# Late feed-forward tiles of a routed decoder block in half tiles of 128 rows, two experts a step, first layer in whole fp32

## The chip, the cores and the metric

One Trainium2 chip, one NeuronCore. The metric is the device time of one execution in microseconds (us), the median of the runs; lower is better.

## The reference

A pre-norm decoder block in fp32 on x of 8 batches x 256 rows x 128 columns: self attention with a hyperbolic distance, cross attention to 512 context rows a batch, and a routed feed-forward. The last part is what matters here:

```python
logits = -dist2 + jnp.einsum('bld,ed->ble', x, rw) + rb
topv, topi = jax.lax.top_k(logits, TOP_K)            # 4 of 16 experts
w = jax.nn.softmax(topv, axis=-1)
hidden = jax.nn.gelu(jnp.einsum('bld,efd->blef', x, w1) + b1, approximate=False)   # 128 -> 512
exp_out = jnp.einsum('blef,edf->bled', hidden, w2) + b2                            # 512 -> 128
sel = jnp.take_along_axis(exp_out, topi[..., None], axis=2)
fused = jnp.sum(w[..., None] * sel, axis=2)
```

Each of the 2048 rows goes to 4 of 16 experts: 8192 (row, expert) pairs. With the reference's own inputs the experts get 795, 395, 564, 125, 242, 518, 21, 542, 789, 908, 478, 25, 1110, 287, 504 and 889 of them (counted on the reference's routing). In tiles of 256 rows, each with one expert, that is 42 tiles; in half tiles of 128 rows it is 73.

## The kernel before, in words

Attention runs first, batch after batch. While cross attention runs, each row is normalised, routed, and sent by POOL's indirect DMAs (L835) into a DRAM table `rows`, which has a region of 2048 rows for each expert; a row there is 130 floats (the row, where its result goes, its weight).

The feed-forward is a walk over `TILES` tiles (L39: 47, the most that any routing can need). Which expert and which start in `rows` a tile has is computed on DVE (`early_map`, `late_map`, `late_starts`) and read into registers by each engine (`tile_entry`). The first nine, `EARLY`, are full tiles of what was sent before the last batch; the others come when the last batch's rows have landed. With the inputs above, 33 of the 38 late tiles (t = 9 to 41) hold rows, and t = 42 to 46 are empty but walked all the same. For each tile t, and two or three tiles deep at once:

- SP, `load_tile` (L581 to L586): waits until the ring slot t mod 6 (`NR` = 6) is free, that is until both result DMAs of tile t-6 have landed (`rout`), reads the start into a register, and issues one DMA of 256 rows into `RIN`, two rows a partition.
- PE, `rows_turn` (L1494): two transposes of 128x128 into `tps`.
- ACT, `x_high` (L1117) and `stage_high` (L1123): the high parts of the rows and of the expert's 128x512 first weights, rounded to fp32r. DVE, `x_low` (L2132) and `stage_low` (L2125): the remainders.
- PE, `hidden` (L1504): 4 chunks x 3 fp32r matmuls (high x high, high x low, low x high) over 256 rows. ACT, `gelus` (L1133): 4 Gelus of 256 columns.
- PE, `outputs` (L1519): 2 x 4 fp32 matmuls of 128 columns; the trace has two MATMUL records for each fp32 matmul (x16).
- DVE, `weigh_out` (L2142, L2145): adds the bias, multiplies by the weight. POOL (L881): two indirect DMAs of 128 rows into the DRAM table `picks`.

The order of the work is written out by hand. PE's step t is: read the expert, transposes of tile t+2, `hidden` of t+1, `outputs` of t. ACT's is `x_high` and `stage_high` of t+1, then `gelus` of t. DVE's is `x_low`, `stage_low` of t+2, then `weigh_out` of t.

The end: SP has issued every `load_tile`, reads six counts of `DONE_I` (`real_tiles`, L599) that say how many tiles hold rows, waits until these tiles' results have landed (L602), and only then loads `picks` back in 16 DMAs (L605). PE and DVE add these to X, and SP writes `out`.

Of the kernel before, what the change touches and what calls it, by code (L numbers as in the profile page):

```python
# [26 lines left out]
P = 128  # L27
# [10 lines left out]
SLOTS = 256  # L38
TILES = (B * N * TOPK + E * (SLOTS - 1)) // SLOTS  # L39
RW = D + 2  # L40
# [52 lines left out]
def decoder_block(nc, a, out):  # L93
    with ExitStack() as ctx:
# [154 lines left out]
        def s_emptied(b, n):  # L249
# [21 lines left out]
        iota_i, iota_f = sB("iota_i", [E], I32), sB("iota_f", [E])  # L271
        step_i, step_f = sB("step_i", [8], I32), sB("step_f", [8])
        first_i, first_f = sB("first_i", [E], I32), sB("first_f", [E])
# [11 lines left out]
        NEXT = sB("NEXT", [E])  # L285
        CNT, CMP, TILE_N, LOW, LOWN, END = (sB("CNT", [E]), sB("CMP", [E, 8]), sB("TILE_N", [E]), sB("LOW", [E, E]),
                                            sB("LOWN", [E, E]), sB("END", [E]))
# [8 lines left out]
        wo_x, less_half = sB("wo_x", [D]), sB("less_half", [1])  # L296
        EARLY = 9

# [170 lines left out]
        def y_bank(t):  # L469

            return (ops[:, :, :].rearrange("p a n -> p (a n)"), bps[:, :])[0 if t < EARLY else t % 2]

        def y_free(t):

            return t if t < EARLY else t - 1

        def tile_row(t):

            return (MAPI[0], t) if t < EARLY else (MAPI[1], t - EARLY)

        def tile_entry(t, c):

            table, at = tile_row(t)
            return table[at:at + 1, c:c + 1]

# [13 lines left out]
        def _(sp):  # L499
# [81 lines left out]
            def load_tile(t):  # L581

                s = t % NR
                wait(sp, rout[s], 32 * (t // NR))
                at = sp.value_load(tile_entry(t, 1), min_val=0, max_val=(E + 1) * CAP - SLOTS)
                sp.dma_start(RIN[:, s], rows[bass.ds(at, SLOTS), :].rearrange("(p i) c -> p i c", i=2)).then_inc(rin[s], 16)  # L586
            for t in range(NR):
# [30 lines left out]
        def _(g):  # L618
# [152 lines left out]
            ch.step(g.iota(iota_i[:, :], pattern=[[1, E]], base=0, channel_multiplier=0))  # L771
            ch.step(g.iota(step_i[:, :], pattern=[[SLOTS, 8]], base=0, channel_multiplier=0))
            ch.step(g.iota(first_i[:, :], pattern=[[CAP, E]], base=0, channel_multiplier=0))
# [111 lines left out]
        def _(act):  # L885
# [233 lines left out]
            def stage_high(t):  # L1119

                e = act.value_load(tile_entry(t, 0), min_val=0, max_val=E - 1)
                wait(act, h_full, 2 * (t - 1))
                act.copy(W1h[:, t % 2, :], W1[:, bass.ds(e * FF, FF)]).then_inc(w1_high, 1)  # L1123
                return e
# [21 lines left out]
            for t in range(TILES):  # L1146
                if 0 < t < TILES - 1 and t != EARLY - 1:
                    x_high(t + 1)
                    at.append(stage_high(t + 1))
                if t == 3:  # L1150
                    t_copy("n3", B - 1)
                if t == 4:
                    half_tanh(B - 1)
                gelus(t, at[t])
                if t == EARLY - 1:
                    act.wait_ge(map_rdy, 2)
                    x_high(t + 1)
                    at.append(stage_high(t + 1))
            for i, (lo, hi) in enumerate(PE_PIECES):
# [4 lines left out]
        def _(pe):  # L1164
# [323 lines left out]
            def rows_turn(t):  # L1488

                s = t % NR  # L1490
                pe.wait_ge(rin[s], 16 * (t // NR + 1))
                wait(pe, x_lo, t - 1)
                for i in range(2):
                    ins = pe.transpose(tps[t % 2][:, i * P:(i + 1) * P], RIN[:, s, i, 0:D], ident[:, :])  # L1494
                ins.then_inc(rows_full, 1)

            def hidden(t):

                pe.wait_ge(x_lo, t + 1)
                pe.wait_ge(w1_low, t + 1)  # L1500
                wait(pe, h_rdy, FC * (t - 1))
                for c in range(FC):
# [7 lines left out]
            def outputs(t, e):  # L1510

                pe.wait_ge(h_rdy, FC * (t + 1))
                wait(pe, y_used, y_free(t))
# [3 lines left out]
                for i in range(2):  # L1517
                    for c in range(FC):
                        ins = pe.matmul(y[:, i * P:(i + 1) * P], HB[:, t % 2, c, i * P:(i + 1) * P],  # L1519
                                        W2[:, bass.ds(e * FC * D + c * D, D)], start=(c == 0), stop=(c == FC - 1))  # L1520
                ins.then_inc(y_full, 1)

            def tile_expert(t):
                return pe.value_load(tile_entry(t, 0), min_val=0, max_val=E - 1)

# [10 lines left out]
            for t in range(TILES):  # L1536
                if t == EARLY:
                    pe.wait_ge(map_rdy, 2)
                e = tile_expert(t)
                if t == EARLY - 1:  # L1540
# [24 lines left out]
        def _(dve):  # L1565
# [298 lines left out]

            def tile_starts(table):

                rch.link(dve.tensor_scalar(MAPF[:, 2:3], MAPF[:, 2:3], float(CAP // SLOTS - 1), float(SLOTS), ALU.min, ALU.mult))
                rch.link(dve.scalar_tensor_tensor(out=MAPF[:, 1:2], in0=MAPF[:, 3:4], scalar=float(CAP),
# [3 lines left out]
            def early_map():  # L1872
# [4 lines left out]
                                                  op0=ALU.add, op1=ALU.subtract))  # L1877
                rch.link(dve.tensor_tensor(CMP[:], CNT[:, :].unsqueeze(2).broadcast_to([P, E, 8]),
                                           step_f[:, :].unsqueeze(1).broadcast_to([P, E, 8]), ALU.is_gt))
                rch.link(dve.tensor_reduce(FULL[:, :], CMP[:], AX, ALU.add))  # L1880
                tile_ends(FULL, END)
# [3 lines left out]
                tile_experts(FULL)  # L1885
                tile_starts(MAPI[0])

            def late_map():

                dve.wait_ge(*t_emptied("pl", B - 1))  # L1890
                rch.link(dve.tensor_tensor(CNT[:, :], NEXT[:, :], first_f[:, :], ALU.subtract))
                rch.link(dve.tensor_tensor(CMP[:], CNT[:, :].unsqueeze(2).broadcast_to([P, E, 8]),
                                           step_f[:, :].unsqueeze(1).broadcast_to([P, E, 8]), ALU.is_gt))
                rch.link(dve.tensor_reduce(TILE_N[:, :], CMP[:], AX, ALU.add))
                rch.link(dve.tensor_tensor(TILE_N[:, :], TILE_N[:, :], TAKEN[:, :], ALU.subtract))
                tile_ends(TILE_N, END)

            def late_starts():
# [4 lines left out]
                rch.link(dve.tensor_reduce(PASTN[:, 0:1], PAST[:, :], AX, ALU.add))  # L1903
                rch.link(dve.tensor_tensor(MAPF[:, 2:3], MAPF[:, 2:3], PASTN[:, 0:1], ALU.add))
                tile_starts(MAPI[1])

            def real_tiles():

                rch.link(dve.tensor_scalar(DONE_F[:, :], END[:, E - 1:E], float(EARLY), None, ALU.add))
                rch.link(dve.tensor_tensor(ORD[:, :], ORD[:, :], DONE_F[:, :].broadcast_to([P, TURNS]), ALU.is_lt))  # L1910
# [218 lines left out]
            def x_low(t):  # L2129
# [3 lines left out]
                                  ALU.subtract).then_inc(x_lo, 1)  # L2133

            def weigh_out(t, e):

                s = t % NR
                dve.wait_ge(rin[s], 16 * (t // NR + 1))
# [3 lines left out]
                dve.tensor_tensor(ROUT[:, s], y_bank(t)[:, 0:2 * D].rearrange("p (i d) -> p i d", i=2),  # L2142
                                  B2B[:, bass.ds(e * D, D)].unsqueeze(1).broadcast_to([P, 2, D]), ALU.add).then_inc(y_used, 1)
                dve.wait_ge(y_used, t + 1)
# [10 lines left out]
            for t in range(TILES):  # L2155
# [3 lines left out]
                if t == EARLY - 1:  # L2159
                    dve.wait_ge(map_rdy, 2)  # L2160
                    x_low(EARLY)
                    at.append(stage_low(EARLY))
                elif t + 2 < TILES and t + 2 != EARLY:
                    x_low(t + 2)
                    at.append(stage_low(t + 2))
                if t == 0:
                    back_at("tr", B - 1)
# [18 lines left out]
                if t == EARLY - 1:  # L2186
                    x_low(EARLY + 1)
                    at.append(stage_low(EARLY + 1))
            for k, (lo, hi) in enumerate(DVE_PIECES):
# [38 lines left out]
```

## Time and profile before

| | |
|---|---|
| time, median of 3 runs | 820.78 us (820.42 to 823.08) |
| the profiled execution's own time | 820.2 us |
| its span in the profile | 818.5 us |
| busy: PE / DVE / ACT / POOL | 701.4 / 648.6 / 581.9 / 524.2 us |
| mean granted TensorE clock | 0.784 of full speed |

A row of the timeline or of the chain begins with its start in the span and its length. "SPq" is SP's queue of instructions, where its DMAs are issued. A length behind a DMA in the chain of waits is the time from issue to landing. `F_RIN` is `RIN`, `F_HB` the Gelu's output, `B_W` either `W` or `W1`. A busy engine in the profile is not one at its peak, since the ends of matmuls are modelled.

### The profile page before, as it was taken

The page shows a single profiled execution, that of the slowest core. Times are in us where ns is not written, and L with a number is a line of the kernel's source. Part 1 is how long each engine was busy: PE and PEld are TensorE (multiplying, and loading weights), DVE is VectorE, ACT ScalarE, POOL GpSimd, SP SyncE. Part 2 cuts the span into 40 slices and gives each one's busy share as a digit, 9 for nine tenths or more (in the row PEclk, how much of TensorE's full clock was granted, in tenths as well). Part 3 has the DMA queues.
Part 4 walks back from the last instruction along what each step waited for, and adds up shares of the span by engine and source line. Part 5 has one row for each costly group of instructions (what it writes and reads, how often), then busy time and mean ns, then how long its engine had stood idle before and what let it go on. Part 6 is the DMA issues. An engine that isn't in the chain of part 4 may idle for free.

```text
span 818.5 us, 17509 instructions
## 1 busy us (share of the span) xinstructions
PE 701.4 (86%) x5760; PEld 474.6 (58%) x5760; DVE 648.6 (79%) x1643; ACT 581.9 (71%) x881; POOL 524.2 (64%) x671
## 2 busy tenths in 40 slices
PE   5456789789887787989999999999989969999996
PEld 3244455456554464545544444454436969999994
DVE  7899999999999899778888898898644845555554
ACT  4427999999999989145767866867756637776771
POOL 4518797787787796442634877876754575666663
PEclk9655555555555555658999999999987979999998
DMA  9990000000000200052061111001323122222228
GB/s 295 336 319 2 1 1 1 1 1 1 0 1 1 75 0 1 1 167 72 2 213 40 41 35 40 24 23 37 89 69 118 50 78 68 81 77 77 80 75 281
DMA packets 58152, 58.78 MB, mean 72 GB/s; under 512 B 9968, under 2 KB 49776, under 8 KB 57936
## 3 DMA queue, kind: packets, MB, share of 16 engines
q1 hardware_dynamic: 53008, 47.24, 19.4%
q0 software_dynamic: 5056, 10.43, 3.8%
q8 instruction: 48, 0.79, 0.4%
q14 instruction: 40, 0.33, 0.1%
HBM read 25.97 MB, written 29.57 MB: 68 GB/s over the span
## 4 chain that ended last, share of the span: by engine, by line
PE 40%; DVE 27%; issue 13%; POOL 11%; DMA 5%; SPq 2%; ACT 2%; DVEq 0%; POOLq 0%; ACTq 0%
DVE S_FB L1682 6%; PE slot L1504 5%; DVE S_YZ L1694 4%; PE ops L1397 4%; PE slot L1209 4%; PE ops L1519 3%; PE slot L1372 3%; PE ops L1232 3%; DVE S_YZ L1715 3%; PE slot L1381 3%; POOL rows L835 3%; POOL B_ROW L462 3%; PE bps L1519 2%; DVE X_junk L1745 2%; POOL picks L881 2%
## 5 line engine op out<-in xcount | busy, mean ns | idle before, releaser
L673 POOL TENSOR_TENSOR S_YZ<-S_YZ 128x512 f32<-128x512 f32 x128 | 183.0, 1463 | 57.2 <-ACT S_YZ L959 57.0
L1011 ACT ACTIVATE B_W<-slot 128x512 f32<-128x512 f32 x256 | 139.0, 595 | 79.0 <-PE slot L1381 78.9
L881 POOL DMA_INDIRECT picks<-F_ROUT,F_GOAL x94 | 103.7, 1103 | 57.3 <-DVE F_ROUT L2145 38.8
L1209 PE MATMUL slot<-S_UQT,S_UKT 32*128 32x256 f32 x256 | 84.4, 474 | 55.9 <-DVE S_YZ L1694 54.8
L1745 DVE CUSTOM_DVE_ANT_0 X_junk<-tps,X_MB 128x512 bf16<-128x512 f32 x165 | 109.9, 688 | 18.3 <-PE tps L1356 15.6
L1209 PEld LDWEIGHTS slot<-S_UQT,S_UKT 32*128 32x128 f32 x256 | 56.3, 297 | 86.1 <-DVE S_YZ L1694 71.5
L1682 DVE TENSOR_SCALAR S_FB<-slot 128x512 f32<-128x512 f32 x128 | 84.6, 683 | 13.1 <-PE slot L1213 12.5
L835 POOL DMA_INDIRECT rows<-B_ROW,B_IDX x64 | 64.6, 1009 | 31.8 <-issue 15.8
L1694 DVE SCALAR_TENSOR_TENSOR S_YZ<-slot,S_FB 128x512 f32<-128x512 f32 x128 | 83.4, 682 | 1.6
L1213 PE MATMUL slot<-S_GQT,S_GKT 32*128 32x256 f32 x256 | 84.3, 445 | 0.0
L1397 PE MATMUL ops<-B_W,X_VX 128*9 128x256 f32 x1024 | 82.4, 397 | 0.0
L1715 DVE SCALAR_TENSOR_TENSOR S_YZ<-S_YZ 128x1024 f32<-128x1024 f32 x50 | 79.7, 1597 | 0.0
L1133 ACT ACTIVATE F_HB<-slot,B_B 128x256 f32<-128x256 f32 x188 | 73.5, 473 | 4.6 <-PE slot L1504 4.6
L1745 DVE CUSTOM_DVE_ANT_0 X_junk<-slot,X_MB 128x512 bf16<-128x512 f32 x91 | 61.9, 687 | 14.6 <-PE slot L1356 13.2
L1381 PE MATMUL slot<-B_QFT,X_KFT 32*128 32x256 f32 x512 | 68.3, 345 | 0.0
L1356 PE MATMUL tps<-X_KFT,X_QFT 24*128 24x512 f32 x165 | 64.5, 533 | 0.4 <-DVE X_MX L1745 0.4
L1372 PE MATMUL slot<-B_MBT,ident_bf 64*64 64x512 bf16 x256 | 59.3, 419 | 3.5 <-DMA B_MBR<-B_MBT 3.5
L1372 PE MATMUL slot<-B_MBR,ident_bf 64*64 64x512 bf16 x256 | 58.4, 419 | 3.9 <-ACT B_W L1011 3.9
L977 ACT ACTIVATE S_YZ<-S_YZ 128x2048 f32<-128x2048 f32 x32 | 61.0, 1909 | 0.5
L1213 PEld LDWEIGHTS slot<-S_GQT,S_GKT 32*128 32x128 f32 x256 | 60.7, 297 | 0.0
L968 ACT ACTIVATE S_YZ<-S_YZ 128x2048 f32<-128x2048 f32 x32 | 60.2, 1904 | 0.2
L1232 PE MATMUL ops<-S_YZ,S_VF 128*9 128x256 f32 x512 | 56.4, 599 | 3.0 <-ACT OT L985 1.9
(340 smaller groups left out, 1783.2 us busy)
## 6 DMA issues: line engine op xcount, KB each, us to landing
rows<-S_blank SPq DMA_DIRECT2D x17, 1040.0 KB, 12.1
F_RIN<-rows SPq DMA_DIRECT2D x47, 130.0 KB, 2.1
B_W<-w1T SPq DMA_DIRECT2D x16, 256.0 KB, 4.8
F_W<-w2T SPq DMA_DIRECT2D x16, 256.0 KB
X_CT<-ctxT SPq DMA_DIRECT2D x8, 256.0 KB, 4.9
B_MBR<-B_MBT SPq DMA_DIRECT2D x16, 128.0 KB, 2.6
B_W<-picks SPq DMA_DIRECT2D x8, 256.0 KB, 8.7
B_W<-picks SPq DMA_DIRECT2D x4, 384.0 KB, 5.9
```

The source lines that it names most:

```text
L673: g.tensor_tensor(Y[:, n % YR], Y[:, n % YR], Zr[:, n % ZR], ALU.add).then_inc(f_rdy, 1)
L881: g.indirect_dma_start(out=picks[:, :], out_offset=bass.IndirectOffsetOnAxis(ap=GOAL[:, s, i:i + 1], axis=0), in_=ROUT[:, s, i, :], in_off ...
L1011: act.activation(W[:, at + i, 2 * j:2 * j + 2, :].rearrange("p t n -> p (t n)"), e_bank(k, i), ACT.Exp, scale=SCALE).then_inc(e_rdy, 1)
L1209: ins = pe.matmul(slot[n % 2][:, 0, kt * N:(kt + 1) * N], UKT[r:r + 32, p, g, kt * P:(kt + 1) * P], UQT[r:r + 32, p, g, :], start=True, st ...
L1213: ins = pe.matmul(slot[n % 2][:, 1, kt * N:(kt + 1) * N], GKT[rg:rg + 32, p, v, kt * P:(kt + 1) * P], GQT[rg:rg + 32, p, :], start=True, s ...
L1372: pe.matmul(e_bank(k, i)[to:to + 64, :], ident_bf[at:at + 64, at:at + 64], src[at:at + 64, p, 2 * j:2 * j + 2, :].rearrange("p t n -> p (t ...
L1381: ins = pe.matmul(e_bank(k, i)[:, tt * N:(tt + 1) * N], KFT[r:r + 32, p, g, t * P:(t + 1) * P], QFT2[r:r + 32, g, :], start=False, stop=(t ...
L1397: ins = pe.matmul(ops[32 * r:32 * r + VW, g % 2, :], VX[:, b % 2, t, h, :], W[:, h % WR, t, :], start=(t == 0), stop=(t == TM - 1))
L1682: dve.tensor_scalar(FB[:, n % FR], slot[n % 2][:, 1, :], 2.0 / DENOM_MIN, None, ALU.min).then_inc(g_rdy, 1)
L1694: dve.scalar_tensor_tensor(out=Y[:, n % YR], in0=slot[n % 2][:, 0, :], scalar=0.0, in1=FB[:, n % FR], op0=ALU.max, op1=ALU.mult).then_inc( ...
L1715: dve.scalar_tensor_tensor(out=Zr[:, n % ZR:n % ZR + 2, :], in0=v, scalar=2.0, in1=v, op0=ALU.add, op1=ALU.mult).then_inc(z_rdy, 1)
L1745: dve.tensor_tensor_reduce(out=junk[:, i, :], in0=bank, in1=MB[:, c % 2, t, :], scale=1.0, scalar=-3.0e38, op0=ALU.add, op1=ALU.max, accum ...
```

## The change

The nine early tiles stay. Behind them a step takes two half tiles of 128 rows, each with an expert of its own. `TILES` falls from 47 to 40: 9 and (61 + 1) / 2 = 31 late steps (L39). With the inputs above the early tiles take 18 of the 73 halves, and the 55 left fill 28 steps (t = 9 to 36); t = 37 to 39 are empty.

In a late step SP reads two starts and issues two DMAs of 128 rows. The first layer is 4 chunks x 2 halves of one fp32 matmul over 128 rows, with no high and low parts: ACT copies the first expert's weights whole (`stage_first`, into the space of `MBT`), DVE the second's (`stage_second`, space of `MBR`) and the rows (`x_whole`, into `OTX`). ACT's `x_high` goes. The Gelus become 8 of 128 columns, DVE's bias add becomes 2 of 128 columns, and PE, ACT and DVE read two experts into registers. POOL's work in a step is the same.

```diff
-TILES = (B * N * TOPK + E * (SLOTS - 1)) // SLOTS
+EARLY = 9
+HALVES = (B * N * TOPK - EARLY * SLOTS + E * (P - 1)) // P
+TILES = EARLY + -(-HALVES // 2)
...
+        WL = [v[:].bitcast(F32).rearrange("p a m n -> p a (m n)") for v in (MBT, MBR)]
+        xL = OTX[:, :, 0, :]
...
+        def rin_count(t):
+            return sum(16 if u < EARLY else 32 for u in range(t % NR, t + 1, NR))
+        def tile_experts_of(eng, t):
+            return [eng.value_load(tile_entry(t, 0, i), min_val=0, max_val=E - 1) for i in range(1 if t < EARLY else 2)]
...
+                for i in range(2):
+                    at = sp.value_load(tile_entry(t, 1, i), min_val=0, max_val=(E + 1) * CAP - P)
+                    sp.dma_start(RIN[:, s, i], rows[bass.ds(at, P), :]).then_inc(rin[s], 16)
...
+            def stage_first(t):
+                e = tile_experts_of(act, t)
+                wait(act, h_full, 2 * (t - 1))
+                act.copy(WL[0][:, t % 2, :], W1[:, bass.ds(e[0] * FF, FF)]).then_inc(w1_high, 1)
+                return e
...
-                    act.activation(HB[:, t % 2, c, :], slot[t % 2][:, c // 2, c % 2 * SLOTS:(c % 2 + 1) * SLOTS],
-                                   ACT.Gelu, bias=B1[:, bass.ts(e, 1), c]).then_inc(h_rdy, 1)
+                    w = SLOTS // len(e)
+                    for i in range(len(e)):
+                        act.activation(HB[:, t % 2, c, i * w:(i + 1) * w],
+                                       slot[t % 2][:, c // 2, c % 2 * SLOTS + i * w:c % 2 * SLOTS + (i + 1) * w],
+                                       ACT.Gelu, bias=B1[:, bass.ts(e[i], 1), c]).then_inc(h_rdy, 1)
...
+                if t >= EARLY:
+                    pe.wait_ge(w1_high, t + 1)
+                    for c in range(FC):
+                        for i in range(2):
+                            at = c % 2 * SLOTS + i * P
+                            ins = pe.matmul(slot[t % 2][:, c // 2, at:at + P],
+                                            WL[i][:, t % 2, c * P:(c + 1) * P],
+                                            xL[:, t % 2, i * P:(i + 1) * P], start=True, stop=True)
...
+            def stage_second(t):
+                e = tile_experts_of(dve, t)
+                dve.wait_ge(h_full, 2 * (t - 1))
+                dve.tensor_copy(WL[1][:, t % 2, :], W1[:, bass.ds(e[1] * FF, FF)]).then_inc(w1_low, 1)
+                return e
+            def x_whole(t):
+                dve.wait_ge(rows_full, t + 1)
+                dve.wait_ge(h_full, 2 * (t - 1))
+                dve.tensor_copy(xL[:, t % 2, :], tps[t % 2][:, 0:SLOTS]).then_inc(x_lo, 1)
...
+                    rch.step(dve.tensor_tensor(ROUT[:, s, 0], y_bank(t)[:, 0:D], B2B[:, bass.ds(e[0] * D, D)], ALU.add))
+                    dve.tensor_tensor(ROUT[:, s, 1], y_bank(t)[:, D:2 * D], B2B[:, bass.ds(e[1] * D, D)], ALU.add
+                                      ).then_inc(y_used, 1)
+                    rch.sync()
```

The maps count in halves behind the early tiles: `late_map` compares 16 experts with 16 steps of 128 rows instead of 8 of 256, `late_starts` and `real_tiles` scale by 2 and 0.5.

On PE, one late step (behind the experts' read): before, two transposes and 12 first-layer matmuls of 256 columns, from the first of which on six are shown (`F_xTh`, `F_W1h` are the high parts, `F_xTl`, `F_W1l` the low ones).

```order
L1524 TENSOR_LOAD B_MAPI
L1524 ISA x2
L1494 MATMUL tps<-ident,F_RIN 128x128 [waits x_lo,rin2]
L1494 MATMUL tps<-ident,F_RIN 128x128
L1504 MATMUL slot<-F_xTh,F_W1h 128x256 [waits h_rdy,w1_low,x_lo]
L1504 MATMUL slot<-F_xTl,F_W1h 128x256
L1504 MATMUL slot<-F_xTh,F_W1l 128x256
L1504 MATMUL slot<-F_xTh,F_W1h 128x256
L1504 MATMUL slot<-F_xTl,F_W1h 128x256
L1504 MATMUL slot<-F_xTh,F_W1l 128x256
```

In the changed kernel, the same place (`B_OT` holds the rows, `B_MBT` and `B_MBR` the two experts' weights; the pair of matmuls stands there four times):

```order
L495 TENSOR_LOAD B_MAPI
L495 ISA x2
L495 TENSOR_LOAD B_MAPI
L495 ISA x2
L1522 MATMUL tps<-ident,F_RIN 128x128 [waits x_lo,rin4]
L1522 MATMUL tps<-ident,F_RIN 128x128
L1535 MATMUL slot<-B_OT,B_MBT 128x128 [waits h_rdy,w1_high,w1_low,x_lo]
L1535 MATMUL slot<-B_OT,B_MBR 128x128
L1535 MATMUL slot<-B_OT,B_MBT 128x128
L1535 MATMUL slot<-B_OT,B_MBR 128x128
```

Twelve matmuls of 256 columns became eight of 128, there are two reads of the table, and the first layer waits for ACT's weights (`w1_high`) too.

On SP, the loads of one ring slot, before:

```order
L585 TENSOR_LOAD B_MAPI [waits rout1]
L585 ISA x2
L586 ISA
L586 DMA F_RIN<-rows 128x260
L585 TENSOR_LOAD B_MAPI [waits rout2]
```

and in the changed kernel:

```order
L602 TENSOR_LOAD B_MAPI [waits rout1]
L602 ISA x2
L603 ISA
L603 DMA F_RIN<-rows 128x130
L602 TENSOR_LOAD B_MAPI
L602 ISA x2
L603 ISA
L603 DMA F_RIN<-rows 128x130
L602 TENSOR_LOAD B_MAPI [waits rout2]
```

A slot's second half is read for and issued behind its first half.

## Rows read from the trace of the kernel before

**Rows 1.** Busy time by stretch: us, PE, PEld, DVE, ACT, POOL, PEclk, DMA share, GB/s

```profile
667.00:672.00 5.00, 5.00 (x24) 5.00 (x25) 2.00 (x6) 1.36 (x3) 3.97 (x4) 0.50 0.33 95
690.00:710.00 20.00, 20.00 (x177) 20.00 (x177) 11.26 (x29) 14.19 (x36) 12.89 (x13) 1.00 0.27 81
```

**Rows 2.** Chain of waits in order of time, one late step

```profile
680.56 0.22 PE tps L1494 x2
680.78 1.43 PE slot L1504 x12
682.21 1.79 PE bps L1519 x16
```

**Rows 3.** Chain of waits, the first late rows' load and the tile behind

```profile
664.68 2.17 DMA F_RIN<-rows
...
667.59 3.42 PE ops L1519 x16
...
671.43 2.07 PE slot L1504 x12
```

**Rows 4.** Chain of waits, one turn of the ring of six slots

```profile
727.00 1.69 PE ops L1519 x15
...
728.82 0.44 DVE F_ROUT L2142
...
732.33 3.11 DMA picks<-F_ROUT,F_GOAL
...
736.17 3.48 DMA F_RIN<-rows
...
739.70 0.44 PE tps L1494 x2
```

**Rows 5.** Timeline, SP, tile 15's load, and L586's DMAs by source line

```profile
683.15 0.34 SPq L586 DMA_DIRECT2D F_RIN<-rows  x1
...
DMA to landing us min/median/max: 2.0/2.1/2.5
```

**Rows 6.** Timeline of ACT, one late step

```profile
691.12 0.37 ACT L1117 CAST F_xTh<-tps 128x256 fp32r<-128x256 f32 x1 [0.65 <-PE tps L1494]
691.84 0.62 ACT L1123 CAST F_W1h<-B_W 128x512 fp32r x1 [0.35 <-PE slot L1504]
692.37 1.56 ACT L1133 ACTIVATE F_HB<-slot,B_B 128x256 f32<-128x256 f32 x4
```

**Rows 7.** ACT by source line and form, 690 to 750 us

```profile
L1133 ACT ACTIVATE F_HB<-slot,B_B x70: 463/471/483, 689.6 to 749.3; 128x256 f32<-128x256 f32 x70
...
L1121 ACTq TENSOR_LOAD <-B_MAPI x17: 279/331/395, 691.1 to 747.1; - x17
```

**Rows 8.** Timeline of ACT at the program's start, copies back to back

```profile
16.44 0.46 ACT L892 COPY S_YZ<-tps 128x384 f32<-128x384 f32 x1
16.79 0.62 ACT L904 CAST HIq<-S_YZ 128x512 fp32r<-128x512 f32 x1
17.31 0.59 ACT L195 COPY S_YZ<-slot 128x512 f32<-128x512 f32 x1
17.79 0.64 ACT L909 ACTIVATE S_HIk<-S_YZ 128x512 fp32r<-128x512 f32 x1
```

**Rows 9.** Timelines of POOL and DVE, and DVE by form

```profile
692.65 1.48 POOL L881 DMA_INDIRECT picks<-F_ROUT,F_GOAL  x1 [0.70 <-DVE F_ROUT L2145]
694.44 0.96 POOL L881 DMA_INDIRECT picks<-F_ROUT,F_GOAL  x1 [0.31 <-issue]
...
692.60 0.69 DVE L2125 TENSOR_TENSOR F_W1l<-B_W,F_W1h 128x512 fp32r<-128x512 f32 x1 [0.37 <-ACT F_W1h L1123]
...
L1923 DVE TENSOR_TENSOR On<-bps,rec 128x128 f32<-128x128 f32 x10 | 2.9, 291 | 0.3
```

**Rows 10.** Tile 40's outputs on the timeline, then the chain to the end

```profile
783.16 1.95 PE L1519 MATMUL ops<-F_W,F_HB 128*128 x16
...
788.65 3.47 DMA picks<-F_ROUT,F_GOAL
...
792.85 0.34 SPq L586
...
796.76 0.33 SPq L605
...
802.33 9.12 DMA B_W<-picks
```

**Rows 11.** The last stretch, by engine (columns as in rows 1)

```profile
800.00:818.50 18.50, 10.32 (x55) 7.33 (x53) 8.92 (x17) 2.28 (x6) 6.29 (x6) 0.84 0.81 282
```

**Rows 12.** Timeline of PE, tile 9's outputs

```profile
675.18 1.95 PE L1519 MATMUL bps<-F_W,F_HB 128*128 x16
```

More of the change, by code:

```diff
@@ L471, in y_bank, with h_count, tile_entry @@
             return (ops[:, :, :].rearrange("p a n -> p (a n)"), bps[:, :])[0 if t < EARLY else t % 2]
+        def h_count(t):
+            return FC * (t + max(0, t - EARLY))
+        def rin_count(t):
+            return sum(16 if u < EARLY else 32 for u in range(t % NR, t + 1, NR))
         def y_free(t):
             return t if t < EARLY else t - 1
[L477 to L483, printed above, removed]
+        def tile_entry(t, c, i=0):
+            table, at = (MAPI[0], t) if t < EARLY else (MAPI[1], 2 * (t - EARLY) + i)
             return table[at:at + 1, c:c + 1]
+        def tile_experts_of(eng, t):
+            return [eng.value_load(tile_entry(t, 0, i), min_val=0, max_val=E - 1) for i in range(1 if t < EARLY else 2)]
         cosh_rdy = sem("cosh_rdy")
@@ L1146, in _ @@
             for t in range(TILES):
-                if 0 < t < TILES - 1 and t != EARLY - 1:
+                if 0 < t < EARLY - 1:
                     x_high(t + 1)
@@ L1153, in _ @@
                     half_tanh(B - 1)
+                if EARLY < t + 1 < TILES:
+                    at.append(stage_first(t + 1))
                 gelus(t, at[t])
@@ L1156, in _ @@
                     act.wait_ge(map_rdy, 2)
-                    x_high(t + 1)
-                    at.append(stage_high(t + 1))
+                    at.append(stage_first(EARLY))
             for i, (lo, hi) in enumerate(PE_PIECES):
@@ L1500, in hidden @@
                 pe.wait_ge(w1_low, t + 1)
-                wait(pe, h_rdy, FC * (t - 1))
+                wait(pe, h_rdy, h_count(t - 1))
+                if t >= EARLY:
[6 more added lines that the diff above has]
+                                            xL[:, t % 2, i * P:(i + 1) * P], start=True, stop=True)
+                        if c % 2:
+                            ins.then_inc(h_full, 1)
+                    return
                 for c in range(FC):
@@ L1903, in late_starts @@
                 rch.link(dve.tensor_reduce(PASTN[:, 0:1], PAST[:, :], AX, ALU.add))
-                rch.link(dve.tensor_tensor(MAPF[:, 2:3], MAPF[:, 2:3], PASTN[:, 0:1], ALU.add))
-                tile_starts(MAPI[1])
+                rch.link(dve.scalar_tensor_tensor(out=MAPF[:, 2:3], in0=PASTN[:, 0:1], scalar=2.0, in1=MAPF[:, 2:3],
+                                                  op0=ALU.mult, op1=ALU.add))
+                tile_starts(MAPI[1], P)
             def real_tiles():
-                rch.link(dve.tensor_scalar(DONE_F[:, :], END[:, E - 1:E], float(EARLY), None, ALU.add))
+                rch.link(dve.tensor_scalar(DONE_F[:, :], END[:, E - 1:E], 0.5, float(EARLY), ALU.mult, ALU.add))
                 rch.link(dve.tensor_tensor(ORD[:, :], ORD[:, :], DONE_F[:, :].broadcast_to([P, TURNS]), ALU.is_lt))
@@ L2160, in _ @@
                     dve.wait_ge(map_rdy, 2)
-                    x_low(EARLY)
-                    at.append(stage_low(EARLY))
-                elif t + 2 < TILES and t + 2 != EARLY:
+                    x_whole(EARLY)
+                    at.append(stage_second(EARLY))
+                elif t + 2 < EARLY:
                     x_low(t + 2)
                     at.append(stage_low(t + 2))
+                elif EARLY < t + 2 < TILES:
+                    x_whole(t + 2)
+                    at.append(stage_second(t + 2))
                 if t == 0:
@@ L2186, in _ @@
                 if t == EARLY - 1:
-                    x_low(EARLY + 1)
-                    at.append(stage_low(EARLY + 1))
+                    x_whole(EARLY + 1)
+                    at.append(stage_second(EARLY + 1))
             for k, (lo, hi) in enumerate(DVE_PIECES):
```

53 lines of the change are left out of this document (29 added, 24 removed).

## The prediction

> **What bounds the kernel now.** I read the busy time by stretch first, then the chain of waits, then the timelines of a late step. From tile 9 on PE is busy all the time at a clock of 1.00, that is 2.4 GHz, while ACT is busy 14.2 of 20 us, POOL 12.9 and DVE 11.3 [rows 1]. A late step is 0.22 us of transposes, 1.43 of first layer and 1.79 of second layer: 3.44 us, and nothing else is in it [rows 2]. So PE sets the pace. Two other clocks are close behind. One is the ring of six slots. The turn in [rows 4] goes from the end of tile 24's outputs (728.69) through DVE, POOL, the results' landing, SP and the load to tile 30's transposes at 739.70: 11.0 us, where PE needs these rows three steps, 10.3 us, after those outputs. The late part has 1.5 us of such stalls: tile 9's outputs start at 675.18 [rows 12], tile 40's at 783.16 [rows 10], 107.98 us for 31 steps, which at 3.436 are 106.5. The other is POOL: 0.70 wait, 1.48, a gap of 0.31, 0.96 [rows 9], together 3.45.
>
> What the end waits for is not PE's last tile. SP issues tile 46's load (792.85) when tile 40's results have landed (788.65 + 3.47 = 792.12), then reads its six counts, and starts to load the results at 796.76 [rows 10]. The last of these lands at 811.45. So I follow one point, the start of L605, 796.76, and what sets it.
>
> **The step.** Removed are 12 fp32r matmuls of 256 columns, 1.43 us [rows 2]. Added are 8 fp32 matmuls, a 128x128 weight against 128 columns. That is exactly the form of the second layer, 8 of them in 1.79 us [rows 2]. A step becomes 0.22 + 1.79 + 1.79 = 3.80 us; I use 3.79. The step gets 0.36 us dearer, but there are fewer: 28 with rows in place of 33.
>
> **ACT**, does it fit in 3.79? The Gelus run at a pitch of (1.56 - 0.47) / 3 = 0.36 us at 256 columns [rows 6, 7]. No row has a Gelu of 128. From above, the pitch stays 0.36. From below, it falls by 0.13, the difference between 384 columns (16.44 to 16.79, 0.35) and 512 (17.31 to 17.79, 0.48) in instructions back to back [rows 8], which gives 0.23. I take 0.255, near the lower end, since those rows are of the same engine, and keep a little for the register instruction ahead of each Gelu. A read of the table costs ACT 0.33 for the load [rows 7] and some 0.2 behind it: from the start of `x_high` to that of `stage_high` there are 0.72 us with one read [rows 6]. With two, I put 1.2 us from the last Gelu's start to the weight copy's, then 0.53 to the first Gelu [rows 6]. ACT's loop is 1.73 + 7 x 0.255 = 3.5 us, below 3.79. At a pitch above (3.79 - 1.73) / 7 = 0.294 ACT sets the pace, and at 0.36 the step is 1.73 + 2.52 = 4.26 us.
>
> A rule speaks against this cut: the Trainium skill, "VectorE: DVE Perf Modes", in its table of costs with errata, gives ScalarE 172 cycles an instruction from PSUM beside one a column, at 1.2 GHz. As an estimate by that page, a Gelu of 256 would be 357 ns, which this trace's pitch of 0.36 agrees with, and one of 128 would be 250 ns: each half pays the fixed part again, and the loop would be 1.73 + 7 x 0.25 = 3.48 us. By the upper bound from the trace it would be 4.26.
>
> **DVE.** `x_low` becomes a copy of as many columns; the weights' subtraction (0.69, rows 9) becomes a copy that I bound by 0.29 to 0.69 and that nothing waits for; ACT's part before it goes. The bias add in two halves is 2 x 0.29 [rows 9] with one wait in place of 0.44 [rows 4], some 0.15 more on the way to POOL. DVE has 8.7 idle of 20 us [rows 1], 1.5 a step, so its second read of the table (0.6) stays covered. PE's second read lies in its queue ahead of the array, under 1.79 us of outputs.
>
> **The ring.** Tile t's slot must be loaded again within three steps of its outputs' end: 10.3 before, 3 x 3.79 = 11.4 us after. Over tiles 15 to 46 (32 loads) I take load issue minus that end: it is 6.0 for the first (683.15 [rows 5] - 677.13 [rows 12]) and 7.7 for the last, and between 6.0 and 8.5, median 6.6. To this come DVE's 0.15 and SP's second half: from landing to issue SP takes 0.73 (792.12 to 792.85, rows 10), and the DMA instruction 0.34, so the second half is issued 1.1 us behind the first. Typically 6.6 + 0.15 + 1.1 + 2.1 for the landing [rows 5] = 10.0, below 11.4; at worst 8.5 + 0.15 + 1.1 + 2.1 = 11.9, 0.5 late, and once in a while a load of 3.48 [rows 4]. Playing the 32 values through the ring in random order gives 1.2 us of stalls (0.2 to 2.4) where the same play for before gives 0.9. So: 1.2.
>
> **The start of the late part.** PE stands still until tile 9's rows have landed [rows 3]. Its second half is issued 1.1 us later: +1.1 on the path. Then the clock is at 0.50, 1.2 GHz, and rises within tile 9's first layer [rows 1, 3]: tile 8's outputs take 3.42, and that first layer 2.07 instead of 1.43. That is the same afterwards. The first layers of tiles 9 and 10 come before tile 9's outputs, each 0.35 dearer: +0.7. `late_map` compares twice as many elements, 0.3 us, but it runs beside POOL's sends, which the load waits for: nothing.
>
> **The end.** Tile 33 is now what the last load waits for, and SP reads its six counts right behind it (3.3 us), three steps before tile 36, the last with rows, is through. So the reads are covered. Before, from tile 40's outputs to L605 it is 796.76 - 783.16 = 13.6 us. After, from tile 36's: 1.95 + 6.6 - 0.73 + 0.15 = 8.0 to landing, 0.2 for the wait's exit: 8.2.
>
> **The sum**, on the start of L605:
> - start of the late part: 1.1 + 0.7 = +1.8
> - steps from tile 9's outputs: before 107.98; after 27 x 3.79 + 1.2 = 103.5: -4.5
> - last outputs to L605: 8.2 - 13.6 = -5.4
> - behind L605, where the DMAs run at 282 GB/s [rows 11]: four result DMAs of 64 KB fewer in the way, 0 to -0.9: -0.4.
>
> Together -8.5 us against the profiled execution's 820.2 (span 818.5), which stands 0.6 below the median of 820.78. Forecast: 812.0 us, between the two bases. PE is no obstacle behind that: L605 starts at 675.18 + 1.8 + 103.5 + 8.2 = 788.7, and PE's empty steps 37 to 39 end at 780.5 + 3 x 3.79 + 1.95 = 793.8, ahead of the landings (the first DVE add waits for one).
>
> **Rivals.**
> - **The ring takes PE's place.** If two DMAs of 128 rows land as the slow load did, 3.5 us, the mean path is 7.0 + 1.25 + 3.5 = 11.75 us, a step of 3.92, and with its scatter 4 to 5 us more in all: 816.5. For it: the path is already over the limit in a few turns [rows 4]. Against: a load of 130 KB lands in 2.0 to 2.5 [rows 5]. 0.2.
> - **ACT becomes the bound, and the kernel slower.** If the Gelu's pitch does not fall with its width, the step is 4.26 us, 27 x 0.47 = 12.7 more: 824.7. The gain is gone from a step of 4.10 on, a pitch of 0.34. For it: each Gelu has a register instruction ahead of it. Against: pitch and width in [rows 8]. 0.09, and 0.05 more for a pitch between, near 820.
> - **POOL is held up by DVE.** POOL's first DMA takes 1.48 when DVE's weight instruction begins just before it and 0.96 otherwise [rows 9]. If the new copy holds both, POOL's step is 0.70 + 1.48 + 0.31 + 1.46 = 3.95 us, 27 x 0.16 = 4.3 more: 816.3. The Trainium skill, "SBUF — State Buffer", on the shared port pair, has a DVE fp32 copy within SBUF hold POOL's descriptor writing for its whole length; this kernel's copy is one such. But one copy a step can hold one of two DMAs, as now. 0.05.
> - **The end does not come earlier**, because SP's counts or the empty steps hold it: then only the steps count, 817. Nothing in the rows speaks for it. 0.02.
>
> **Numbers.** The forecast as summed has 0.59, with 809.5 to 814.5 from its stalls, the last item and the landing. 0.3% is 2.5 us, about what a measurement of this kernel can tell from no change: faster means below 818.3. Faster: forecast, ring and POOL less their tails, 0.83. Same 0.07, slower 0.10. The range, 809.5 to 819.0, takes in ring and POOL and leaves ACT's upper bound out.
>
> **What would show it.** PE fully busy from tile 9, at a step of 3.8 us with 16 slot records in 1.79; eight Gelus at a pitch near 0.25; idle time on ACT; L605 first at about 788.7; six reads of the counts before tile 36 lands. Wrong it is if PE waits for Gelus (ACT), for loads (ring), if the half tile's first layer takes more than 1.8 us, or if L605 starts later than 791.

## The result, and the profile after

The changed kernel takes **812.29 us** (median of 18 runs, 810.4 to 818.14), the kernel before, run beside it, 822.63 us (18 runs, 817.07 to 826.32). The ratio is 0.9897 with a 95% interval of 0.9873 to 0.9920: some 8.5 us less, where the medians are 10.3 us apart. A ratio and its interval come from each kernel's runs within 1.5% of its fastest, a median from all of them. The profiled execution took 810.4 us, its span is 808.6 us, its mean granted TensorE clock 0.781.

From the page of the changed kernel, the span and the busy times:

```profile
span 808.6 us, 17944 instructions
PE 690.2 (85%) x5674; PEld 462.2 (57%) x5674; DVE 627.6 (78%) x1639; ACT 574.8 (71%) x932; POOL 498.5 (62%) x657
```

Every engine lost busy time, PE 11.2 us of it and POOL 25.7. Then the busy time by stretch (columns as in [rows 1]):

```profile
667.00:672.00 5.00, 4.07 (x19) 4.07 (x20) 0.94 (x3) 0.00 (x0) 3.78 (x5) 0.50 0.38 105
690.00:710.00 20.00, 20.00 (x181) 20.00 (x181) 9.11 (x32) 14.78 (x47) 10.59 (x11) 1.00 0.27 74
```

Against [rows 1], PE is as full as before and the clock is again 1.00 (2.4 GHz). ACT has 0.6 us more, DVE 2.2 and POOL 2.3 less. The chain of waits shows the late part from its first load on (start, length, what; left out are SP's register instructions and waits):

```profile
664.90 0.34 SPq L603
...
666.00 1.88 DMA F_RIN<-rows
...
667.93 0.69 PE tps L1522 x2
668.62 3.42 PE ops L1558 x16
672.03 0.43 PE tps L1522 x2
672.46 2.32 PE slot L1535 x16
674.78 0.22 PE tps L1522 x2
675.00 1.79 PE slot L1535 x16
676.78 1.79 PE bps L1558 x16
```

A step is 0.22 + 1.79 + 1.79 us. By PE's timeline, where [rows 12] are from too, tile 9's outputs start at 676.62 and tile 36's at 779.60; the chain cuts at the modelled ends, some 0.16 later. The same view at the other end, from tile 36's outputs to the load of the results:

```profile
779.76 1.80 PE ops L1558 x16
...
783.47 0.97 POOL picks L898
...
784.74 2.23 DMA picks<-F_ROUT,F_GOAL
...
786.99 0.33 SPq L622
...
791.80 8.12 DMA B_W<-picks
...
799.94 0.70 DVE X L2253
```

This answers to [rows 10]: the counts are no longer between the landing (786.97) and SP's first load, which starts at 786.99 instead of 796.76. ACT's and POOL's timelines for one step, the idle time before each row in brackets:

```profile
703.23 2.17 ACT L1159 ACTIVATE F_HB<-slot,B_B 128x128 f32<-128x128 f32 x8 [0.80 <-PE slot L1535]
705.61 0.62 ACT L1147 COPY B_MBT<-B_W 128x512 f32 x1 [0.21 <-issue]
707.02 2.17 ACT L1159 ACTIVATE F_HB<-slot,B_B 128x128 f32<-128x128 f32 x8 [0.80 <-PE slot L1535]
```

```profile
700.06 0.97 POOL L898 DMA_INDIRECT picks<-F_ROUT,F_GOAL  x1 [1.55 <-DVE F_ROUT L2203]
701.33 0.97 POOL L898 DMA_INDIRECT picks<-F_ROUT,F_GOAL  x1 [0.30 <-issue]
```

ACT waits 0.80 us a step for PE, and POOL 1.55 where it had 0.70 [rows 9]. PE alone sets the pace now: from tile 10's outputs on, each of the 26 steps takes 3.79 us.

Where the 9.9 us between the two profiled spans (818.5 and 808.6) went, by the same three points in each:

| | before | after | change | forecast |
|---|---|---|---|---|
| start of tile 9's outputs | 675.18 | 676.62 | +1.4 | +1.8 |
| to the last outputs' start (31 and 27 steps) | 107.98 | 102.98 | -5.0 | -4.5 |
| to the first load of results | 13.60 | 7.39 | -6.2 | -5.4 |
| to the end of the span | 21.7 | 21.6 | -0.1 | -0.4 |

### The profile page after: what moved, and what is told of

It is laid out like the page before. It is cut to its first block, busy times and chain, and to the rows that moved or that the text cites. A ratio compares the mean times of both kernels' runs of the same rounds, so it can differ in the third digit from the quotient of the medians.

```text
span 808.6 us, 17944 instructions
## 1 busy us (share of the span) xinstructions
PE 690.2 (85%) x5674; PEld 462.2 (57%) x5674; DVE 627.6 (78%) x1639; ACT 574.8 (71%) x932; POOL 498.5 (62%) x657
## 4 chain that ended last, share of the span: by engine, by line
PE 44%; DVE 28%; issue 13%; POOL 9%; DMA 3%; ACT 2%; SPq 1%; DVEq 0%; POOLq 0%; ACTq 0%
PE slot L1535 6%; DVE S_FB L1718 6%; DVE S_YZ L1730 4%; PE ops L1425 4%; PE ops L1558 4%; PE slot L1237 4%; PE bps L1558 3%; DVE S_YZ L1751 3%; PE slot L1400 3%; POOL rows L852 3%; PE ops L1260 3%; PE slot L1409 3%; POOL B_ROW L465 3%; DVE X_junk L1781 3%; PE bps L1274 2%
## 5 line engine op out<-in xcount | busy, mean ns | idle before, releaser
L898 POOL DMA_INDIRECT picks<-F_ROUT,F_GOAL x80 | 77.7, 971 | 69.5 <-DVE F_ROUT L2203 52.1
L1159 ACT ACTIVATE F_HB<-slot,B_B 128x128 f32<-128x128 f32 (+1 forms) x284 | 81.5, 394 | 37.0 <-PE slot L1535 33.6
L1718 DVE TENSOR_SCALAR S_FB<-slot 128x512 f32<-128x512 f32 x128 | 84.5, 683 | 13.9 <-PE slot L1241 13.2
```

What stands on the lines that cost most here:

```text
L1718: dve.tensor_scalar(FB[:, n % FR], slot[n % 2][:, 1, :], 2.0 / DENOM_MIN, None, ALU.min).then_inc(g_rdy, 1)
```

## The experiments

Ten runs of nine other kernels, beside two repetitions of the changed one. Two things are needed to read them. The runs were made on several chips: a1, e3b, e8 and e9 on one, e2, e5, e6 and e7 on another, where before takes 820.4 and 820.7 us, close to the main result's 822.6 (whose chip isn't on record), and a0, e1, e3 and e4 on a slow one, where it takes 874.0. And the late part starts anywhere from 667 to 674 us on the other chips, in both kernels, since the attention before it varies. So the late part is told by differences within one execution: T is the start of the first late transposes, Z that of SP's first load of results. Before has T 666.90 and Z 796.76, 129.9 us apart; after has 667.93 and 786.99, 119.1 apart.

**Repetitions.** a0 and a1 are the changed kernel again.

> The changed kernel once more, as the mark for the runs beside it. Theory (fewer, dearer steps on a PE that stays the bound; the end waits for tile 36): 0.99 of before, L622 first issued near 787 us in its span. Rival (the gain was chance between two groups of times): a ratio between 0.995 and 1.0.

> The changed kernel once more, beside the three runs of this call. Theory: 0.99 of before where ACT is not held up, and no gain where it is (seven stops of up to 4.4 us with no semaphore to wait for, as in the run before).

a1: 811.89 us against 820.42, ratio 0.9899 (0.9852 to 0.9947), T 668.96, Z 787.6. The gain repeats. a0 ran on the slow chip: 870.4 us against 874.04, ratio 0.9991 (0.9950 to 1.0031). **No gain can be told there.** The clock falls further in its attention part (0.74 to 0.93 between 400 and 700 us), which both kernels share. But from 740 us on it is at 1.00, and still Z - T is 134.1 us, 15 longer: 5.4 of it ahead of tile 9's outputs, 8.5 in the 27 steps, 1.1 at the end. In the start SP's register instructions take 0.7 us each where after has some 0.04, so that tile 10's second load is issued 5.3 us behind T and not 0.6 (a0's chain of waits):

```profile
716.03 0.69 SPq L603
...
718.34 1.86 DMA F_RIN<-rows
```

In the steps it is ACT that stands. Its waits by line (740 to 845 us: total, times, longest) and a row of its timeline, of a0:

```profile
ACT F_HB L1159 <- remote: 13.9, 5, 4.4
ACT F_HB L1159 <- issue: 4.0, 1, 4.0
```

```profile
786.82 2.18 ACT L1159 ACTIVATE F_HB<-slot,B_B 128x128 f32<-128x128 f32 x8 [3.66 <-remote]
```

Every 21 to 25 us ACT stands for some 4 us ahead of the Gelus, with nothing in the profile that it waits for, and PE waits for these Gelus right behind (the last row: its second layer starts at 789.15). The eight Gelus themselves take 2.18 us, where after has 2.17, so it is no slower instruction. e1, on the same chip, has no such stop on ACT between 730 and 850 us (its longest wait there is 1.8 us), but DVE has one of 4.2 us in the last steps, on the chain to the end:

```profile
866.07 0.42 DVE L2168 TENSOR_TENSOR F_ROUT<-bps,F_B2B 128x256 f32<-128x256 f32 x1 [4.22 <-remote]
```

What stops SP, ACT and DVE on this chip stays open, and so does what the kernel before loses by it there, since no profile of it was taken on that chip. That the changed kernel's ACT has more instructions (932 against 881) was a guess that no run tested.

**e1: whole fp32 with the tiles as they were.** The kernel before; behind tile 9 ACT copies weights and DVE rows whole, and the first layer is one fp32 matmul of 256 columns a chunk.

```diff
+                if t >= EARLY:
+                    for c in range(FC):
+                        ins = pe.matmul(slot[t % 2][:, c // 2, c % 2 * SLOTS:(c % 2 + 1) * SLOTS],
+                                        WL[0][:, t % 2, c * P:(c + 1) * P], xL[:, t % 2, :], start=True, stop=True)
+                        if c % 2:
+                            ins.then_inc(h_full, 1)
+                    return
```

> The kernel before with one part of the change alone: the late tiles stay tiles of 256 rows and one expert, but the first layer is one fp32 matmul over 256 rows for each chunk, on weights copied whole by ACT and rows copied whole by DVE; the weights' and rows' low parts go. Theory (PE sets the pace and the fp32 first layer costs 0.36 us a step, so that the halves alone give the gain): a step of 3.79 us, 31 steps to tile 40's outputs are 11.0 us longer, less up to 1.5 of ring stalls, plus 0.7 at the start: 10 us slower than before, about 830. Rival (the lighter load on ACT and DVE is what gave the time): no slower than before, or faster. For POOL: its first result DMA of a step is 0.97 instead of 1.48 us if the weights' subtraction with two SBUF inputs held it up; it stays at 1.48 if the cause lies elsewhere.

883.47 us (4 runs) against 874.04, on the slow chip: 9.4 us slower by the medians, 14 (9 to 19) by the ratio, 1.0162 (1.0103 to 1.0221). Its trace gives the part that is not that chip's stops: each of the 31 steps from tile 9's outputs to tile 40's takes 3.73 us, 115.7 in all where before took 107.98, so 7.7 us more: steps dearer by 9.1 in all, less the 1.5 that before's ring stalled. The theory had 3.79 a step. Chain of waits:

```profile
790.06 1.73 PE slot L1516 x8
791.79 1.78 PE ops L1538 x16
793.58 0.22 PE tps L1504 x2
```

The fp32 first layer takes 1.73 us in four matmuls of 256 columns, 1.79 in eight of 128: cutting in halves costs PE 0.06 us a step, whole fp32 costs 0.30. By itself this part of the change is a loss. Half tiles with the high and low parts kept were not run, so what halving alone brings is told from this step and the tile counts. And POOL's first DMA, 1.48 us in [rows 9], is back at 0.97 with no weight instruction on DVE at all (ACT copies the weights); the two longest, of 1.19 and 1.20 us, lie beside an early tile's subtraction. POOL's late DMAs by source line (count, then min/median/max ns), of before and, in the second fence, of e1:

```profile
L881 POOL DMA_INDIRECT picks<-F_ROUT,F_GOAL x57: 963/967/1482, 680.2 to 778.3; - x57
```

```profile
L883 POOL DMA_INDIRECT picks<-F_ROUT,F_GOAL x44: 957/966/1195, 682.6 to 778.9; - x44
```

**e2: the counts ahead of the last load**, in the kernel before.

```diff
-            for t in range(EARLY, TILES):
+            for t in range(EARLY, TILES - 1):
                 load_tile(t)
             sp.wait_ge(done_rdy, 1)
             used = [sp.value_load(DONE_I[s:s + 1, 0:1], ...) for s in range(NR)]
+            load_tile(TILES - 1)
```

> The kernel before, but SP reads the six counts before it loads the last tile instead of behind it. Theory of the end (tile 40's results gate the last load, then 3.3 us of reads run in the open, while tile 41's results land near 795.5): L605 starts 0.7 to 1.3 us earlier, and no more, since tile 41 gates it then; the whole 1 us faster. Rival (the reads alone cost 3.3 us, and so were a large part of the change's gain at the end): 3 us or more faster.

822.35 us, ratio 1.0011 (0.9978 to 1.0044): nothing. Yet Z - T fell from 129.9 to 125.9 us, 1.1 of it fewer ring stalls and 2.8 the counts. So the reads were worth what the rival said, not 0.7 to 1.3 us, and the whole kept none of it. What came behind Z grew from 21.7 to 23.9. The chain of waits of e2 says why:

```profile
807.47 1.80 PE ops L1520 x16
...
810.21 0.69 DVE X L2193
```

It no longer goes through the results' DMAs. DVE adds the results to X (L2193) behind its part of tile 46, so the end waits for the walk's last, empty step. There are **two ends**, and the later one counts: Z + 21.5 us, and the last tile's transposes + 22.4 us (800.8 to 823.2 here). Before sits close to both: its last transposes are at 795.4, 23.1 ahead of its end, so the walk's end is only 0.7 us short of it. After has its last at 781.5, 27.1 ahead.

**e6: a ring of seven slots**, in the kernel before (`NR` = 7, `TURNS` divided by 7).

> The kernel before with seven ring slots instead of six. Theory (the late part had 1.5 us of ring stalls and the last load of tile 46 then waits for tile 39, so that the reads are covered): tile 40's outputs start 1.5 us earlier, L605 2 to 2.5 us earlier, the whole 2 us faster. Rival (POOL's 3.45 us a step is the true pace of before, and the ring only shows it): no faster, and POOL falls behind PE.

819.25 us, ratio 0.9985 (0.9954 to 1.0016). All stalls are gone (each step 3.43 or 3.44 us), so the rival of POOL as the pace is out. Z - T is 125.4, and again nothing is won, where the theory had 2 us: PE's transposes by source line end at 800.4, and the span, 822.7 us, ends 22.3 behind them.

```profile
L1494 PE MATMUL tps<-ident,F_RIN x86: 272/273/477, 642.1 to 800.4; 128*128 128x128 f32 x86
```

**e5: a ring of five slots**, in the changed kernel (`NR` = 5, `TURNS` divided by 5), to measure a slot's turn: from the end of a tile's outputs to the landing of the rows that take its slot.

> The changed kernel with five ring slots. Theory (a slot's turn is 6.4 us from outputs to load, 1.25 for DVE's second add and SP's second half, 1.9 to landing, 9.6 us in all, against two steps): PE waits for rows, a step of 4.8 us, 27 x 1.0 = 27 us slower than the changed kernel. Rival (the turn is shorter, 8 us, because POOL is no longer near its limit): a step of 4.0, 6 us slower.

833.1 us (a single run), and Z - T is 137.3, 18.2 longer, between the theory's 27 and the rival's 6. Steps are 3.8 to 5.3 us, 4.5 in the mean, so a turn, which now has two steps, is 9.0 us. PE waits for loads (total, times, longest), and one turn in the chain of waits:

```profile
PE tps L1522 <- DMA F_RIN<-rows: 13.3, 18, 1.3
```

```profile
739.90 1.69 PE ops L1558 x15
...
743.50 0.97 POOL picks L898
...
744.77 2.27 DMA picks<-F_ROUT,F_GOAL
...
748.86 2.04 DMA F_RIN<-rows
```

From the outputs' end, 741.59, to the landing, 750.90, 9.3 us, in this turn. Three steps of 3.79 leave 2 us of room.

The stalls of e5 also move POOL's work against DVE's, and some of POOL's DMAs now start while DVE copies the second expert's weights. From the timelines of POOL and DVE:

```profile
694.30 1.22 POOL L898 DMA_INDIRECT picks<-F_ROUT,F_GOAL  x1 [0.30 <-issue]
```

```profile
694.25 0.43 DVE L2177 COPY B_MBR<-B_W 128x512 f32 x1 [0.97 <-PE slot L1535]
```

Nine of e5's DMAs start inside a copy. One that starts 0.05 us into it takes 1.22 us, one at 0.08 into it 1.19, at 0.15 1.11, at 0.21 1.05, at 0.27 1.00, and the four from 0.34 on 0.96 to 0.97 again. So the copy does hold POOL, as the subtraction does.

**e3, e3b: no empty steps**, in the changed kernel: `TILES = 37`, which is enough for the reference's inputs and not for every routing.

> The changed kernel with TILES = 37, so that the three empty steps 37 to 39 are not walked (enough for these inputs alone). Theory (the empty steps lie beside the loads of the results, whose DMAs set the end): L622 starts as in the changed kernel (787), and the whole is the same to 1 us faster. Rival (the walk to the last step sets the end): 3 us or more faster.

> The changed kernel with TILES = 37 once more. Theory (from the loads' start to the end there are 21.6 us with three empty steps and 19.7 without on the chip of the first try, because their DMAs and adds are in the way): L622 at the same time as in the changed kernel, the whole 1.9 us faster. Rival (that difference was the chip's): the same.

On the slow chip 867.61 us, ratio 0.9938 (0.9894 to 0.9983); on a1's chip 808.6 against 820.42, ratio 0.9863 (0.9813 to 0.9913), 3.3 us below a1 by the medians of six runs each, which scatter by 6 to 8 us: no telling from the theory's 1.9. In e3b Z - T is 118.4, in a1 118.6, but from Z (786.0) to the end (806.1) it is 20.1 us instead of 21.3 (a1) or 21.6 (after). On the slow chip it is 19.7 against 21.6 in a0. So the three empty steps cost 1.2 to 1.9 us behind Z. I take it that their result DMAs are in the way of the loads; that was not tried by itself.

**e4: both starts read ahead of the DMAs**, in the changed kernel, the first pair ahead of the wait for the sends.

```diff
+            first = starts(EARLY)
             for s in sent:
                 sp.wait_ge(s, 16 * TN * TOPK * (B // 2))
-            for t in range(EARLY, TILES):
+            load_tile(EARLY, first)
+            for t in range(EARLY + 1, TILES):
```

> The changed kernel, but SP reads both starts of a step before it issues its two DMAs, and the first late step's starts before it waits for the last batch's rows. Theory (the two loads of tile 9 on SP are on the path that starts the late part, 0.73 us for each read and 1.1 between the DMAs): the first late transposes begin 1.4 us earlier, and the whole is 1.4 us faster than the changed kernel. Rival (the start is set by something else, such as the clock or tile 8's outputs): no difference.

869.31 us on the slow chip, ratio 0.9927 (0.9879 to 0.9976), where a0 has 870.4. In the chain of waits the sends land at 717.39, and the two loads follow at once:

```profile
715.25 2.14 DMA rows<-B_ROW,B_IDX
...
717.75 0.34 SPq L607
...
718.14 0.34 SPq L607
```

The transposes start at 720.23, 2.8 us behind the sends' landing where after, on another chip, has 3.9 (664.05 to 667.93). e8 and e9 below, on one chip, have 4.0 and 2.9. So the late start does hold 1.1 us of register reads; what the whole kernel gains by it can't be told apart from that chip's scatter.

**e7, e8: more full tiles ahead.** The changed kernel with `EARLY` = 11 or 10, a ring of 7, half tiles counted as with 9, so that any routing still fits, and the banks of the second layer taken by `(t - EARLY + 1) % 2`: 42 and 41 steps.

```diff
-EARLY = 9
-HALVES = (B * N * TOPK - EARLY * SLOTS + E * (P - 1)) // P
+EARLY = 10
+HALVES = (B * N * TOPK - 9 * SLOTS + E * (P - 1)) // P
...
-        NR = 6
+        NR = 7
```

> The changed kernel with eleven early tiles of 256 rows instead of nine, seven ring slots, and 42 steps in all, so that any routing still fits (early tiles that no expert can fill are empty). Theory (PE stands still for 7 us until the last batch's rows have landed, and two more early tiles of 3.4 us fit there, though tile 11's slot comes free only when POOL has sent tile 4's results, near 667.5): two steps of 3.79 us less behind the standstill, 3 us lost to the slot, 4 to 5 us faster than the changed kernel. Rival (POOL's queue of sends and results sets the late start, and grows by two tiles): no faster.

> The changed kernel with ten early tiles, seven ring slots and 41 steps (banks of the outputs shifted by one, so that they still alternate). Theory (with eleven, tile 11's slot hung on POOL's results of tile 4, which stand behind the last batch's sends; tile 10's slot hangs on tile 3's, which are ahead of them): the first late transposes stay near 668, one step of 3.79 us is gone, the last step walked ends where it did (31 late steps), so the whole is 3 us faster than the changed kernel. Rival (the tenth early tile does not fit in the standstill, or the walk to the empty tiles' end holds the end back, as with eleven): less than 1 us.

e7: 811.85 us, ratio 0.9894 (0.9859 to 0.9929), no better than the change, where the theory had 4 to 5 us. Its first late transposes come at 672.32, and its last ones at 787.0, 22.5 ahead of the end: the walk's end holds it, as the chain of waits shows.

```profile
794.42 1.91 PE bps L1558 x16
...
797.39 0.69 DVE X L2253
```

e8: **807.64 us** (806.4 to 812.6), ratio 0.9834 (0.9788 to 0.9879), 4.2 us below a1, which ran beside the same runs of before (six runs each), and with e9 the best of those that hold for any routing. T is 670.62, Z 784.9, and the chain goes through the results again, with the last transposes 783.2, 23.2 ahead of the end:

```profile
782.64 2.24 DMA picks<-F_ROUT,F_GOAL
...
784.94 0.33 SPq L622
...
795.03 0.77 DVE X L2253
```

Z - T is 114.3, 4.3 below a1's, of which one late step less is 3.8. A seventh slot can bring little by itself here, since the ring of six never stalled in after (see below). **e9** is e8 with e4's edit.

> As the kernel with ten early tiles, and SP reads both starts of a step before its two DMAs, those of the first late step before it waits for the last batch's rows. Theory: 1.4 us faster than with ten early tiles alone, since the first late transposes begin that much earlier and the chain from there on is PE's. Rival (the early tiles' last outputs or the clock set the late start): no difference.

808.36 us, ratio 0.9845 (0.9797 to 0.9893), the same as e8. T is 670.39, only 0.2 earlier: from the sends' landing to T it is 2.9 us instead of 4.0, but in that execution the sends landed 0.9 us later (667.47 against 666.57). The sends in e8's chain of waits, and the first late loads in e9's timeline:

```profile
664.06 2.51 DMA rows<-B_ROW,B_IDX
```

```profile
667.66 0.86 SPq L607 DMA_DIRECT2D F_RIN<-rows  x2
```

What e4's edit is worth in the whole stays unsettled.

## Why the prediction was right, point by point

The time (812.0 against 812.29 us) and the mechanism held. PE sets the pace at the forecast step, and the gain lies about half in the steps and half in the end. That the two times agree to 0.3 us is luck: the forecast was -8.5 us on the trace, which shows -9.9, with three of the four terms off by 0.4 to 0.8 us the same way, and the runs of the changed kernel alone scatter by 8 us. The terms, by the prediction's own steps:

- **The step**, 3.79: shown. 0.22 + 1.79 + 1.79, and over 27 steps 102.98 us = 27 x 3.79 + 0.65, where the 0.65 is no stall of the ring (below). e1 splits it: whole fp32 alone makes a step 0.30 us dearer, so it is the smaller number of steps that pays, and fp32 is its price.
- **ACT**: the pitch is (2.17 - 0.377) / 7 = 0.256 us by the rows below (forecast 0.255). The rival of a pitch that does not fall with the width is out. The Trainium skill, "VectorE: DVE Perf Modes", in its table of costs with errata, has 172 cycles beside one a column; the estimate from it was 0.25, and this trace agrees. Mis-sized was the time with two reads of the table, 1.2 us from the last Gelu's start to the copy's: it is 0.6 (2.17 - 0.377 to the last start, 705.61 for the copy). So ACT's loop is 2.99 us, not 3.5. The Gelus and the table's loads in ACT's queue, by source line:

```profile
L1159 ACT ACTIVATE F_HB<-slot,B_B x151: 358/377/412, 699.7 to 769.5; 128x128 f32<-128x128 f32 x151
...
L495 ACTq TENSOR_LOAD <-B_MAPI x43: 275/285/392, 689.8 to 769.4; - x43
```

- **DVE**: the weights' copy, bounded by 0.29 to 0.69, is 0.43 us, and POOL's DMA keeps its 0.97 in all 67 late ones of after (962 to 975 ns). DVE's timeline, to set against POOL's rows at 700.06 above:

```profile
700.43 0.43 DVE L2177 COPY B_MBR<-B_W 128x512 f32 x1 [0.80 <-issue]
```

  The rival in which this copy makes POOL the pace is out, but for another reason than its mechanism: POOL's first DMA starts 0.37 us ahead of the copy, and no late DMA of after starts while the copy runs. Where one does, it is held, as e5 shows: 1.22 us. The Trainium skill, "SBUF — State Buffer", on the shared port pair, has such a copy block POOL's descriptor writing; e5's trace agrees in kind, with 0.25 us more for a DMA 0.05 us into a copy of 0.43. It is the order of the starts that decides in before too: the DMA at 692.65 starts 0.05 us into the subtraction and takes 1.48 [rows 9], while those that start ahead of a subtraction, or within 0.04 us behind its start, take 0.97.
- **The ring**: no stall at all, forecast 1.2 (0.2 to 2.4). This term was mis-sized. The turn is 9.0 to 9.3 us (e5), not 10.0. The results land in 2.4 us by the median where before had 2.7, POOL's first DMA is 0.5 shorter, and each half lands in 1.8 to 2.1. The rival that two smaller DMAs land later is out. What the steps did lose, 0.6 us, is in the first one, and 0.5 of it is PE's second read of the table, which was put under the outputs at no cost. That holds for the later steps, but in tile 9's the read comes late. PE's timeline, and the queue's reads by source line from 677.9 to 679 us (count, min/median/max ns, first and last start):

```profile
678.92 0.41 PE L1522 MATMUL tps<-ident,F_RIN 128*128 128x128 f32 x2 [0.35 <-issue]
```

```profile
L495 PEldq TENSOR_LOAD <-B_MAPI x1: 301/301/301, 678.2 to 678.2; - x1
```

  The outputs end at 678.57, and the register instructions behind that read only at 678.76. In a1 the same step loses 0.2.
- **The start**: +1.4, forecast +1.8. The second issue comes 1.10 us behind the first, as forecast, but its half lands in 1.88 us instead of 2.17 [rows 3]. Tile 9's first layer takes 2.32 at the rising clock, 0.25 more than before, not 0.35. And 0.2 of the +1.4 is none of the change: the last sends landed at 664.05 instead of 663.82.
- **The end**: -6.2, forecast -5.4. The mechanism is as told: the six reads are done at 781.5, ahead of the last landing at 786.97, which takes 4.6 us off (the last load and the reads). The other 1.6 are POOL's 0.97 instead of 1.46 and a landing of 2.23 instead of 3.47, less the second add.
- **Behind Z**: -0.1, forecast -0.4, but the reason was only half seen. e3 and e3b show that the empty steps that are left still cost 1.2 to 1.9 us there.

What the text did not see is the walk's end. It followed one point, the start of L605, as if a microsecond there were one at the end. In before that is not so: e2 moved it by 2.8 us of counts, e6 by those and by the stalls, and neither won anything, since the walk's last step ends only 0.7 us earlier. In the change the steps are fewer as well (40 for 47), so both ends moved, Z by 9.8 us and the last transposes by 13.9, and the sum came out. PE's empty steps were looked at for the changed kernel only, where they are indeed no obstacle (781.5 + 22.4 = 803.9, ahead of 808.6). And the forecast holds for the chips on which before takes some 821 us: on the slow one no gain can be told, which no rival named.

## What to carry to other kernels

Price an edit against every chain that ends near the end, not the longest alone: of two ends 1 us apart, taking 3 us off one gives nothing, and an edit that shortens both gives all. A more costly instruction pays where it lets the work be cut so that padding falls away; count steps times step, and weigh each part alone, since here one part alone lost 7.7 us over 31 steps, and the whole gained 8.5. A ring or a queue with room to spare is measured by taking a slot away, not by the trace of the kernel that never waits for it. And that two instructions on different engines do not hold each other in one trace can be a matter of which starts first: look for a run in which they start the other way round.

## What the runs showed of the hardware

- POOL's indirect DMA takes 0.97 us. One that starts while DVE runs a 128x512 fp32 instruction on SBUF operands takes longer: 1.22 at 0.05 us into a copy of 0.43 (e5), 1.48 at 0.05 into a subtraction of 0.69 [rows 9]. One that starts ahead of either, or within 0.04 us behind the subtraction's start, takes 0.97.
- An fp32 matmul of 256 columns is 0.43 us, two of 128 are 0.45: so halving the width costs 0.02 us a pair.
- Two loads of 65 KB land in 1.9 us each by the median where one of 130 KB took 2.1 [rows 5].
- The same kernel takes 821 us on some chips and 874 on another. In a0, on the latter, ACT stops for some 4 us every 21 to 25 us with nothing in the profile to wait for, and PE waits for it; the 27 steps take 8.5 us longer. How much of the missing gain this makes was not measured apart.
